# Six warming products instead of twelve, and the first weights loaded and split as k's half, then q's half

## What is computed

```python
x = _layernorm(x + _L0_attn_ref(x, W_qkv, b_qkv, W_proj, b_proj))
x = _layernorm(x + _L0_xattn_ref(x, ctx, ctx, mask, wq, bq, wk, bk, wv, bv, wo, bo))
x = _layernorm(x + _L0_ffn_ref(x, W_qkv, b_qkv, W_gate, b_gate, W_experts, b_experts))
# attention: 16 heads of 16 features
qkv = x @ W_qkv + b_qkv
attn = softmax(mask(einsum('bhqd,bhkd->bhqk', q, k) / 4))
z = einsum('bhqk,bhkd->bhqd', attn, v)
# last layer, beside its attention
gate = softmax(x @ W_gate + b_gate); top_g, top_i = top_k(gate, 2)
moe = einsum('bsef,bse->bsf', einsum('bsd,edf->bsef', x, W_experts) + b_experts, combine)
```

## Time and profile before

| what | value |
|---|---|
| median of 3 runs | 892.40 us (891.79 to 892.42) |
| the profiled execution: time, span | 893.21 us, 891.4 us |
| busy share: PE, DVE, ACT, POOL | 97%, 85%, 66%, 47% |
| granted TensorE clock, mean over the span | 0.993 |

### The profile page before, as it was taken

The page is one execution under the profiler, slowest core; times in us unless marked ns, Lnnn a source line. Parts: engine busy times, 40 slices in busy tenths (PEclk is TensorE's granted clock), DMA queues, the critical chain, the costliest instruction groups (busy, mean ns, idle before and its releaser), DMA issues.

```text
span 891.4 us, 28532 instructions
## 1 busy us (share of the span) xinstructions
PE 866.1 (97%) x10018; PEld 746.3 (84%) x10018; DVE 758.7 (85%) x3509; ACT 585.7 (66%) x1211; POOL 416.8 (47%) x588
## 2 busy tenths in 40 slices
PE   7899999999999999999999999999999999999996
PEld 4788888888888888989888888888888888888874
DVE  4689988998988898888888988888888888888895
ACT  4688888788878787887877644444445554555533
POOL 7688887888864545354444421122222222222201
PEclk8999999999999999999999999999999999999998
DMA  5756655664545454444434222222333333323201
GB/s 183 206 158 167 178 146 156 169 176 131 165 119 144 121 147 131 115 128 113 129 98 121 79 57 60 68 67 72 85 85 85 85 85 85 85 73 84 74 25 61
DMA packets 98268, 100.58 MB, mean 113 GB/s; under 512 B 10704, under 2 KB 90704, under 8 KB 98128
## 3 DMA queue, kind: packets, MB, share of 16 engines
q1 hardware_dynamic: 98128, 98.77, 40.6%
HBM read 18.25 MB, written 4.19 MB: 25 GB/s over the span
## 4 chain that ended last, share of the span: by engine, by line
PE 78%; issue 8%; POOL 5%; ACT 4%; DVE 2%; DMA 2%; SPq 1%; ACTq 0%; POOLq 0%; DVEq 0%
PE work L512 42%; PE work L655 9%; PE max_scores L609 8%; PE scores L632 8%; PE work L664 4%; PE scores L635 3%; PE work L537 1%; ACT attn L815 1%; PE work L673 1%; POOL attn L1156 1%; DMA k_stack<-k_parts 1%; POOL k_parts L1105 1%; POOL rstd L1147 1%; POOL q_parts L1105 1%; DMA k_stack<-in_vo 1%
## 5 line engine op out<-in xcount | busy, mean ns | idle before, releaser
L815 ACT ACTIVATE attn<-scores 128x512 f32<-128x512 f32 x384 | 214.9, 600 | 124.0 <-PE scores L632 111.1
L982 DVE CUSTOM_DVE_ANT_0 max_scores<-max_scores,mask_qk 128x128 f32<-128x128 f32 x872 | 222.9, 325 | 30.3 <-PE max_scores L609 29.3
L1098 POOL TENSOR_TENSOR q_full<-q_full,q_parts 128x512 f32<-128x512 f32 x48 | 55.9, 1166 | 274.2 <-ACT q_parts L773 274.2
L609 PE MATMUL max_scores<-k_stack,q_stack 126*128 126x128 bf16 x1536 | 142.4, 220 | 2.7 <-DMA k_stack<-k_parts 1.6
L632 PE MATMUL scores<-q_stack,k_stack 128*128 128x128 bf16 x1536 | 137.1, 220 | 3.4 <-DMA q_stack<-neg_max_t 1.6
L1057 DVE SCALAR_TENSOR_TENSOR x_all<-work,combine,x_all 128x256 f32<-128x256 f32 x256 | 121.8, 481 | 18.0 <-PE work L512 13.4
L985 DVE TENSOR_REDUCE neg_max<-max_scores 128x4 f32<-128x512 f32 x166 | 111.0, 682 | 24.1 <-PE max_scores L609 16.2
L609 PEld LDWEIGHTS max_scores<-k_stack,q_stack 126*128 126x128 bf16 x1536 | 98.1, 97 | 33.0 <-issue 18.7
L982 DVE DVE_READ_ACCUMULATOR2_ANT neg_max<- 128x1 f32 x872 | 122.9, 141 | 0.0
L632 PEld LDWEIGHTS scores<-q_stack,k_stack 128*128 128x128 bf16 x1536 | 98.1, 97 | 26.4 <-ACT attn L815 8.1
L512 PE MATMUL work<-split_hi,w_hi 128*128 128x256 f32 x384 | 113.2, 295 | 3.2 <-DVE split_lo L884 3.2
(11 more groups left out here) (126 smaller groups left out, 2020.5 us busy)
## 6 DMA issues: line engine op xcount, KB each, us to landing
k_stack<-k_parts SPq DMA_DIRECT2D x288, 128.0 KB, 2.5
q_stack<-q_parts SPq DMA_DIRECT2D x288, 128.0 KB, 2.5
in_t<-in_xt SPq DMA_DIRECT2D x16, 256.0 KB, 3.0
x_all<-in_x SPq DMA_DIRECT2D x16, 256.0 KB, 3.2
in_t<-in_ct SPq DMA_DIRECT2D x16, 256.0 KB, 2.7
out<-x_all SPq DMA_DIRECT2D x16, 256.0 KB, 2.2
stage<-in_e SPq DMA_DIRECT2D x4, 512.0 KB, 4.6
stage<-in_qk SPq DMA_DIRECT2D x2, 512.0 KB, 5.0
```

Of the source, the lines that this page charges most:

```text
L609: mm = pe.matmul(dst[:, b, h2, :], head(QS, n, 2 * p + h2, b, ROWS), head(KS, n, 2 * p + h2, b, ROWS), start=(b + h2 == 0), stop=(b + h2 = ...
L815: act.activation(attn("exp", n, p)[:, :, :], SS[g % 2][:, :, :, :].rearrange("k b h q -> k (b h) q"), ACT.Exp).then_inc(probs_done, 1)
L982: ins = dve.tensor_tensor_reduce(scores, scores, MQ[l][:, :], -1.0, HUGE, ALU.add, ALU.min, NM[n % 2][:, b, h:h + 1])
L1098: pool.tensor_tensor(FULL[x][:, :, :], FULL[x][:, :, :], PART[x][:, 0, :, :], ALU.subtract).then_inc(rest_done[x], 1)
```

## The change

Two things are changed. The loop of warming products runs 3 times instead of 6 (each pass shows as two products in the trace, so 6 instead of 12). And the load of `qk0` is cut by columns: k's half first, then the first item's input, then q's half, each half with its own semaphore, its own copy on ACT (128x512 values instead of 128x1024) and its own subtraction on DVE. In a half, a partition's two rows of 256 values are 1 KB each and no longer lie together. The v and output weights stay one load; what needs them now waits for the third low part instead of the second.

```diff
@@ semaphores and parts
-        first_loaded = [sem(f"first_loaded{j}") for j in range(2)]
+        first_loaded = [sem(f"first_loaded_{name}") for name in ("k", "q", "vo")]
+        FIRST_PARTS = [(FIRST[0][:, :, D:2 * D], D, D), (FIRST[0][:, :, 0:D], 0, D), (FIRST[1], 2 * D, 2 * D)]
@@ SyncE
-            sp.dma_start(FIRST[0], t["qk0"]).then_inc(first_loaded[0], 16)
+            sp.dma_start(FIRST[0][:, :, D:2 * D], t["qk0"][:, :, D:2 * D]).then_inc(first_loaded[0], 16)
             sp.dma_start(IN[0][:, :, :], t["xt"][0]).then_inc(in_loaded[0], 16)
+            sp.dma_start(FIRST[0][:, :, 0:D], t["qk0"][:, :, 0:D]).then_inc(first_loaded[1], 16)
...
-            sp.dma_start(FIRST[1], t["vo0"]).then_inc(first_loaded[1], 16)
+            sp.dma_start(FIRST[1], t["vo0"]).then_inc(first_loaded[2], 16)
@@ TensorE
-            for _ in range(6):
+            for _ in range(3):
                 pe.matmul(WB[WORK_BANKS - 1][0:QUAD, :], VA[0][:, 0, 0:QUAD], VA[0][:, :, 0:2 * P], start=True, stop=True)
@@ output_bias, and v of item 0
-                    pe.wait_ge(first_lo, 2)
+                    pe.wait_ge(first_lo, 3)
@@ feature_major (q and k)
                 if n == 0:
-                    pe.wait_ge(first_lo, 1)
+                    pe.wait_ge(first_lo, 1 if x == "k" else 2)
@@ ScalarE
-            for j in range(2):
+            for j, (src, o, width) in enumerate(FIRST_PARTS):
                 act.wait_ge(first_loaded[j], 16)
-                act.activation(WH0[:, :, j * 2 * D:(j + 1) * 2 * D], FIRST[j], ACT.Copy).then_inc(first_hi, 1)
+                act.activation(WH0[:, :, o:o + width], src, ACT.Copy).then_inc(first_hi, 1)
@@ VectorE
-                o = j * 2 * D
-                dve.tensor_tensor(WL0[:, :, o:o + 2 * D], FIRST[j], WH0[:, :, o:o + 2 * D].bitcast(F32),
+                src, o, width = FIRST_PARTS[j]
+                dve.tensor_tensor(WL0[:, :, o:o + width], src, WH0[:, :, o:o + width].bitcast(F32),
                                   ALU.subtract).then_inc(first_lo, 1)
...
             first_low(0)
             x_low(0, 0)
+            first_low(1)
             dve.wait_ge(bias_loaded, 16)
             dve.tensor_scalar(QBI[:, :, :], COLB[:, :, 0, :], SCALE, None, ALU.mult).then_inc(q_bias_done, 1)
-            first_low(1)
+            first_low(2)
@@ GpSimd, q_low of item 0
-                    pool.wait_ge(first_lo, 2)
+                    pool.wait_ge(first_lo, 3)
                     clear_stacks(STACKS - 1)
```

## The result

The changed kernel is slower: 894.86 us median (893.46 to 896.02, 8 runs) against 891.55 (888.94 to 892.84, 8 runs) of the kernel before, a ratio of 1.0036 (95% interval 1.0024 to 1.0048), or 3.2 us. The forecast was 893.0 us with a range to 894.4. The profiled execution took 896.02 us, its span is 894.3 us. Lines stand two or three further down than in the kernel before (L514 for L512, L877 for L875, L886 for L884).

A forecast was written before the change was run, and what follows sets the result against it. The chain through the v and output weights and DVE's set-up to TensorE was taken as the bound. POOL's +0.4 and the landing's +0.5 made 0.9 us, counted as +0.6 on 892.4: 893.0 us, range 890.6 to 894.4.

The forecast's parts named there:

- What bounds the kernel: First 60 us: the chain enters by the v and output weights, then DVE's set-up, then TensorE, busy 97% of the span.
- Part 2: k of item 0 on TensorE: starts at 6.39; the 2.66 us gain becomes idle time, growing from 3.2 to 4.5 us.
- Rival A: Earlier k and q of item 0 reach the end: 891.0 us (chance 0.07) or 889.7 us (chance 0.07).
- Part 5: Landing of the v weights: later by 0.5 us, between 0 and 1.8, from later issue, short rows and item 2's input.
- Part 4: DVE's set-up held by POOL's earlier operations: +0.4 us at item 1's low part, bounds -2.4 to +1.2.
- The load of item 2's input, my 0.1: Issued at about 5.8 instead of 7.17, while the v weights are in flight: 0.1 us, bounds 0 and 0.7.
- Part 1: Warming products on TensorE: six fewer end at 6.39 instead of 9.05, 2.66 us less; lost warming costs nothing.
- Part 3: ACT's k_full and the POOL steps behind it: at most 1.35 us earlier, worth 0 to the end.
- The sum: Item 1's low part 0.9 us late, of which +0.6 reaches the end: 892.4 + 0.6 = 893.0 us.
- rival D: Clock: if some executions before keep it through the gap, the longer gap takes 2.6 us, 895.0 us; chance 0.04.
- rival C: v weights late by the full 1.8 us plus 0.4 of POOL: 2.2 us, 894.6 us; chance 0.06.
- The list of what the profile should show: First 26 us: k of item 0 near 6.4, idle gap 4.5 us or more, clock 0.50, first max_scores 0.4 to 1 later.

The follow-up runs named there:

- packed_halves: The changed kernel with k's and q's halves as tensors of their own, one 2 KB row per partition instead of two of 1 KB: 893.92 us, ratio 1.0022.
- one_load: The changed kernel with q and k loaded by one transfer as before, halves cut only on ACT and DVE: 893.59 us, ratio 1.0010.
- six_only: The kernel before with 3 passes of warming products instead of 6, nothing else: 893.47 us, ratio 1.0015.
- cut_only: The changed kernel with its 12 warming products back: 895.30 us, ratio 1.0038.
- item2_late: The changed kernel with the load of item 2's input held until the v and output weights' low part is done: 895.09 us, ratio 1.0036.
- one_load_late: one_load with the load of item 2's input held until the v and output weights' low part is done: 893.26 us, ratio 1.0017.
- fill_after: The changed kernel with 3 passes of the warming product ahead of the output bias and 5 behind it: 892.91 us, ratio 1.0009.
- fill_before: The kernel before with 3 more passes of the warming product right behind layer 0's output bias: 891.34 us, ratio 0.9990.
- six_fill: six_only with 5 passes of the warming product behind the output bias: 890.97 us, ratio 0.9987.
- six_item1_early: item1_early with six warming products (3 passes): 889.96 us, ratio 0.9976.
- item1_early: The kernel before with item 1's input copied and its low part made right behind item 0's, ahead of the v weights: 891.49 us, ratio 0.9994.

## Why the prediction was wrong

**What bounds the kernel: right.** The trace of the changed kernel enters the chain by the v and output weights, as the one before did, and the gain of k and q (Part 2) became idle time of TensorE. Rival A never appeared.

**Part 5, the landing of the v weights: the term that was mis-sized.** I took +0.5, with bounds of 0 and 1.8, and the trace has +2.25. I priced the later issue at one issue of 0.46 and hoped that it was hidden; it was 1.25 us, since a load of 256 rows takes SP 0.57 to 0.72 us (and so did the two issues beside them that had not changed), and nothing hid it. The short rows I priced as transfer time only. packed_halves undoes the rows alone and has the landing at 9.36; 0.78 of the 1.30 us between is the issue (4.39 against 3.61), and the other 0.5 is flight, which scatters by more than that. That the cut of the transfer costs time is shown by one_load against the changed kernel (1.0010 and 1.0036); how much of it is rows and how much is one transfer more is not. The load of item 2's input, my 0.1, is 0.3 to 0.5 in the traces and nothing in the times. Over the five traces with the cut load the landing is at 10.0 in the mean (10.66, 10.48, 10.20, 9.67, 9.10), 1.5 us over the mean of the eight with the old loads: the profiled execution of the changed kernel was the latest of them. The sentence of the Trainium skill (DMA: Bandwidth & Descriptors, specifications) that 512 bytes are enough for line rate would have made the term smaller still. Here rows of 1 KB cost more by the issues, of which that rule does not speak.

**Part 4, DVE held by POOL: right.** +0.4 in the changed kernel and in six_only, by three holds of 0.8 to 1.0 us. One reading in it was a little off: 0.27 us is what a memset of 128x256 takes (L907), while a tensor operation of that size took 0.43 when nothing held it (L911), so L912 was held for 0.8 us, not 1.0.

**Part 1 and Part 3: wrong, without weight for the time.** I read the rise of the clock off one trace, inside the first six products. In the ten traces with six products these took anything from 4.30 to 5.33 us, and 5.33 in the changed kernel's, so k of item 0 started at 7.20 and not at 6.39; TensorE had to wait afterwards in any case. ACT's steps do not come 1.35 us earlier but 0.8 later, because the late v weights stand ahead of them.

**The sum and rival D.** k of item 1 started 2.66 us late (2.25 by the landing, 0.4 by POOL), where the sum had 0.9: that is rival C, and beyond its 2.2. I let the slip come through by half or whole and gave the longer idle gap no price in the forecast, and a chance of 0.04 as a rival. It has a price: with the gaps filled and the clock up, six_only gains 2.5 us and the changed kernel 2.4, the kernel before 0.9. That rival D is the reason, that is, that some executions of the kernel before keep the clock through their 3.2 us gap, is likely but not shown. Three groups of runs of the kernel before, 96 in all, give each run's mean granted clock: 21 had 0.997 or more, and these took 890.9 us in the mean, the other 75 took 892.6. Of the 61 runs of the six kernels with more idle time there and no filling (six_only, cut_only, packed_halves, one_load, item2_late, one_load_late) none had 0.997, nor had any of the 8 of the changed kernel (highest 0.993). This mean is a rough mark: it also takes in the last 6 to 9 us of the span, where every trace is at 0.50, and of the 36 runs with filled gaps only 24 reach 0.997. The group means go the same way: 0.997 with the gaps filled, 0.995 for the kernel before, 0.994 for the six kernels, 0.992 for the changed one. No trace of the kernel before that kept the clock is on record.

Between fill_after (1.0009) and fill_before (0.9990) 1.7 us remain, which is the landing and the 0.4 of POOL, and that leaves some 1.5 of the 3.2 us to the clock. The split is rough, since a difference of two such figures is uncertain by 1.5 us or more; that both shares are there is shown, the first by one_load against the changed kernel, the second by six_fill against six_only (0.9987 and 1.0015) and by fill_after against the changed kernel (1.0009 and 1.0036). six_fill and fill_before end 0.3 us apart, so with the gap filled six products in place of twelve cost nothing that could be measured.

**The list of what the profile should show.** Only the clock of 0.50 and the place of entry came true. k_full started at 11.64 (9.5 to 10.5 was forecast), the landing was at 10.66 (8.4 to 9.4), k of item 1 at 19.76 (17.5 to 18.5), the first max_scores 2.1 us late (0.4 to 1), and TensorE's idle time of 4.5 us or more fell into two gaps, 2.75 and 3.81.

## What to carry to other kernels

A load that is cut so that a piece arrives sooner delays all loads behind it when the pieces have shorter and more rows: count the rows, and look which of the later loads the chain hangs on. An idle gap of TensorE can cost more than its length, by the clock that falls behind it: here starting earlier only made the gap longer and the kernel 1.3 us slower, 0.4 of it by DVE's waits (six_only), and products put into the gap gave 2.5 us back (six_fill). And before speeding up a step, move what the chain really ends in: here the low part of item 1's input stood behind set-up work that it does not need, and with that moved the kernel with six products is 2.1 us faster than the kernel before (0.9976), which neither edit alone was (1.0015 and 0.9994).

## What was not expected of the hardware

- SP's issue of a 256 KB load took 0.40 us with 128 rows of 2 KB, and 0.57 to 0.72 with 256 rows of 1 KB; the unchanged loads issued just behind a cut one took 0.57 and 0.60 instead of 0.41 and 0.43.
- The flight of the same 512 KB load, issued at 3.14, varied from 4.78 us (six_item1_early) to 6.32 (one_load) between traces.
- In the first products the record of the granted clock says 1.00 while they are 0.86 us apart, twice the 0.43 they take later: before the clock's first change the spacing tells its level, the record does not. The changed kernel's trace shows it, first two weight loads of warming products, then the stretch:

```profile
2.80 0.18 PEld L520 LDWEIGHTS work<-v_ones 128*32 128x32 f32 x1 [0.68 <-issue]
3.65 0.18 PEld L520 LDWEIGHTS work<-v_ones 128*32 128x32 f32 x1 [0.68 <-issue]
```

```profile
0.00:6.00 6.00, 4.06 (x5) 0.90 (x6) 1.34 (x2) 2.54 (x3) 5.41 (x9) 1.00 0.53 153
```

- The clock did not fall at the same place in each trace. In the changed kernel's and in item2_late's it fell behind a gap of 2.8 us, at 14.0 and 12.7, while the output bias ran; in cut_only's only at 20.0, when k of item 1 had begun behind a gap of 4.72 us; in item1_early's at 23.9, behind one of 1.89 us. With the gaps filled (fill_before, six_fill, fill_after) it stayed up until the last 9 us of the span.
